# First attention of a two-layer kernel: scores as 32-row matmul tiles in pairs of PSUM banks

## The chip, the cores and the metric

The kernel runs on one core of one Trainium2 chip. The metric is device time in microseconds (us): the median of three runs before the change is 1856.27 us (1856.07 to 1857.29). TensorE is called PE below (its weight loads PEld), VectorE DVE, ScalarE ACT, GpSimd POOL. PSUM has eight banks here, each 128 partitions by 512 float32, addressed as `ps[:, bank, column]`.

## What is computed

Two transformer layers over x of 2048 tokens by 128 channels. Only the first sublayer is touched by the change, causal attention with 16 heads of 8 channels:

```python
q, k, v = (qkv[0], qkv[1], qkv[2])
q = _rms_norm(q, q_norm_w)
k = _rms_norm(k, k_norm_w)
q, k = _rope(q, k, cos, sin)
attn = jnp.einsum('bhqd,bhkd->bhqk', q, k) * scale
attn = jnp.where(causal, -jnp.inf, attn)
attn = jax.nn.softmax(attn, axis=-1)
out = jnp.einsum('bhqk,bhkd->bhqd', attn, v)
out = out.transpose(0, 2, 1, 3).reshape(Bc, Tc, C)
return out @ w_proj.T
```

It is followed by a linear frequency-domain layer, a linear attention, and a second softmax attention over experts (8 heads of 64 channels, not causal). Each adds its result to x.

## The kernel before

The tokens are 16 tiles of 128 (`NT`), in 4 chunks of 512 (`NC`, `CH`, `TPC` = 4 tiles a chunk). The 16 heads are taken in 4 groups of 4 (`NG`, `GH`). A head of 8 channels is staged into 32 columns: the value rounded, the rest that rounding left, and one column for the negated row maximum (`stageq`, `stagek`); four heads fill 128 columns. PE transposes a chunk of them into a bank and ACT copies it out (steps `k`, `q`, `q2`).

For queries one copy to `qT` is enough: head h lies in partitions 32h to 32h+31. Keys are copied to `kM[g % 2]`, which has a plane of 128 partitions for every head. Only the head's own 32 partitions hold values; the other 96 are zero, written once by POOL (`kM0`, `kM1`), so that a matmul over all 128 partitions gives the scores of one head. The copy takes four ACT instructions of 32 partitions (L862).

Every score is computed twice. The step `max` (L606, mask L609) computes scores of 128 queries by up to 512 keys, and DVE takes their maximum (L1074) into `mxp`; `m` combines them and `q2` transposes the queries again with the maximum in them. Then `S` (L623, mask L626) computes scores with keys in the partitions, two heads into two banks, and ACT takes exp of both banks in one instruction (L875) into `pbuf0`; `V` (L638) multiplies with the values, four heads in four 32-column tiles of PE into bank 6, each as two passes (float32); `O` copies bank 6 out, `F` transposes it, and DVE divides by the denominator. The causal mask is added by a bfloat16 matmul with the identity, one for each diagonal 128x128 block.

A unit is one `S` with its exp: 128 keys by up to 512 queries of two heads. There are 80 units a group, 320 in all: 192 off the diagonal with 512 columns, and 128 on it, with 512, 384, 256 or 128 columns (32 each). The `max` steps are 560: 384 off the diagonal with one 512-column matmul each, and 176 on it with 256 matmuls.

The order on all engines comes from one list, `SEQ0`, that `merge` builds: the units at their places, `V` for two units four units later, and the preparation for the coming group at places that `paced` interpolates. Each engine runs its own steps of that list strictly in order, with semaphore waits between them. Of the PSUM banks, `S` has 0 to 3 (two pairs in turn, `NS` = 2), bank 6 (`ACC`) gathers `V`, and `RING` = 4, 5, 7 is taken in turn by all else: the `max` steps, all transposes, `pj`, `mix`, `lin`. Before PE fills a bank, `take` waits until the step that had it last has been read. The second attention uses the same ring under the names `ring1` and `SEQ1`.

Chunk by chunk, as the last group ends, the steps `at`, `pj`, `sd`, `ln`, `lt`, `mix`, `sd2`, `ln2`, `lt2`, `lin`, `ex`, `el` carry the projection, the frequency layer and the inputs of the linear attention.

Of the kernel before, what the change touches and what calls it, by code (L numbers as in the profile page):

```python
# [25 lines left out]
ALU = mybir.AluOpType  # L26
# [23 lines left out]
RING = (4, 5, 7)  # L50
# [7 lines left out]
def preparation0():  # L58
# [5 lines left out]
    for g in range(NG):  # L64
# [7 lines left out]
        for c in range(NC):  # L72
# [69 lines left out]
class Ring:  # L142


    def __init__(self, seq, by_dve, by_act):
        self.turn, self.read, self.by_act, self.order = {}, {}, by_act, []
        counts = {True: 0, False: 0}
        for step in seq:
            if step[0] in by_dve + by_act:
                a = step[0] in by_act  # L150
                counts[a] += 1
                self.turn[step], self.read[step] = len(self.order), counts[a]
                self.order.append(step)

    def bank(self, step):
        return RING[self.turn[step] % len(RING)]


def build(nc, A):
    ctx = ExitStack()  # L160
    with ctx:
# [36 lines left out]
        masksb = s0("masksb", [P, 2, P], BF16)  # L198
# [38 lines left out]
        kM0 = s0("kM0", [P, GH, T], F32R)  # L237
        rotating = ExitStack()
        tmp = sbuf(rotating, "tmp", [P, NT, 2 * H0, D0])
        rotating.close()  # L240
        kM1 = s0("kM1", [P, GH, T], F32R)
        kM = (kM0, kM1)
# [71 lines left out]
        s_read1a = sem("s_read1a")  # L314
        s_m = sem("s_m")
# [96 lines left out]
        ring0 = Ring(SEQ0, ("max", "F", "pj", "mix", "lin"), ("k", "q", "q2", "at", "lt", "lt2"))  # L412
        ring1 = Ring(SEQ1, ("proj", "max", "F", "y"), ("t", "q2", "zt"))
# [123 lines left out]
        def _(pe):  # L537
# [32 lines left out]
            def take(ring, step):  # L570

                turn = ring.turn[step]
                if turn >= len(RING):
                    wait_read(pe, ring, ring.order[turn - len(RING)])
                return ring.bank(step)

# [7 lines left out]
            for step in SEQ0:  # L584
# [13 lines left out]
                elif kind == "max":  # L598
                    _, g, c, i, b, h, n = step
                    bank = take(ring0, step)  # L600
                    wait_read(pe, ring0, ("q", g, c))
                    wait_read(pe, ring0, ("k", g, b))
                    w = P * (i + 1) if b == c else CH
                    for a in range(n):
                        it = TPC * c + i
                        mm = pe.matmul(ps[:, bank, w * a:w * (a + 1)], qT[:, g % 2, P * it:P * (it + 1)],  # L606
                                       kM[g % 2][:, h + a, CH * b:CH * b + w], start=True, stop=b < c)
                        if b == c:
                            mm = pe.matmul(ps[:, bank, w * (a + 1) - P:w * (a + 1)], identb[:], masksb[:, 0, :],  # L609
                                           start=False, stop=True)  # L610
                    mm.then_inc(s_turn0, 1)
                elif kind == "S":
# [3 lines left out]
                    if u >= NS:  # L616
                        pe.wait_ge(s_exp, u - NS + 1)
                    wait_read(pe, ring0, ("q2", g, c))
                    wait_read(pe, ring0, ("k", g, c))
                    for i in range(2):  # L620
                        h = 2 * (u % 2) + i
                        b = 2 * (u % NS) + i
# [203 lines left out]
        def _(act):  # L826
# [22 lines left out]
            for step in SEQ0:  # L849
                kind = step[0]  # L850
                if kind in ("k", "q", "q2"):
# [5 lines left out]
                    if kind == "k":  # L857
                        if g == 1:
                            act.wait_ge(s_pconst, 2)
                        for h in range(GH):  # L860
                            rows = slice(32 * h, 32 * h + 32)
# [585 lines left out]
```

## Time and profile before

| | |
|---|---|
| time, median of 3 | 1856.27 us |
| span of the profiled execution | 1857.2 us |
| PE busy | 1645.3 us (89%) |
| DVE busy | 1435.4 us (77%) |
| POOL busy | 878.0 us (47%) |
| ACT busy | 782.5 us (42%) |
| chain that ended last, by engine | PE 66%, DVE 19%, issue 7%, POOL 5%, ACT 2% |
| of it, lines of the first attention | L606 8%, L623 7%, L638 7%, L581 5% |

The profiled execution's own time is its span, 1857.2 us, within 1 us of the median. Busy time of a PE matmul runs from its start to a modelled end, and the next one starts before that end; what a matmul costs is therefore the distance from its start to the next start. The exps of the first attention run from 74.4 us (unit 0) to 625.6 us (unit 319); the rest of the span, from there on, is work that the change leaves as it is.

### The profile page before, as it was taken

The page shows a single profiled execution, that of the slowest core. Times are in us where ns is not written, and L with a number is a line of the kernel's source. Part 1 is how long each engine was busy: PE and PEld are TensorE (multiplying, and loading weights), DVE is VectorE, ACT ScalarE, POOL GpSimd, SP SyncE. Part 2 cuts the span into 40 slices and gives each one's busy share as a digit, 9 for nine tenths or more (in the row PEclk, how much of TensorE's full clock was granted, in tenths as well). Part 3 has the DMA queues.
Part 4 walks back from the last instruction along what each step waited for, and adds up shares of the span by engine and source line. Part 5 has one row for each costly group of instructions (what it writes and reads, how often), then busy time and mean ns, then how long its engine had stood idle before and what let it go on. Part 6 is the DMA issues. An engine that isn't in the chain of part 4 may idle for free.

```text
span 1857.2 us, 26270 instructions
## 1 busy us (share of the span) xinstructions
PE 1645.3 (89%) x8612; PEld 999.3 (54%) x8612; DVE 1435.4 (77%) x2387; ACT 782.5 (42%) x1046; POOL 878.0 (47%) x906
## 2 busy tenths in 40 slices
PE   3899999999999672699899899899999899899997
PEld 2555555555554361566466466466565565565554
DVE  4996785785786369888888888888898888988862
ACT  3457557567556320223433434334334234234441
POOL 2710000000000024358678589589588587687654
PEclk9799999999999775889899999999999999999996
DMA  2000000000000000000000000000000000000000
GB/s 58 1 1 1 1 1 1 1 1 1 1 1 1 11 1 11 0 11 1 11 1 2 11 1 1 11 1 1 12 1 1 11 1 1 1 1 1 1 11 13
DMA packets 12224, 9.34 MB, mean 5 GB/s; under 512 B 3840, under 2 KB 11584, under 8 KB 12096
## 3 DMA queue, kind: packets, MB, share of 16 engines
q1 hardware_dynamic: 12096, 7.66, 1.5%
q8 instruction: 77, 1.26, 0.3%
q14 instruction: 51, 0.42, 0.1%
HBM read 6.61 MB, written 1.05 MB: 4 GB/s over the span
## 4 chain that ended last, share of the span: by engine, by line
PE 66%; DVE 19%; issue 7%; POOL 5%; ACT 2%; SPq 0%; DMA 0%; DVEq 0%; POOLq 0%; ACTq 0%
PE ps L786 10%; PE ps L606 8%; PE ps L623 7%; PE ps L638 7%; PE ps L759 6%; PE ps L581 5%; PE ps L775 4%; PE ps L776 4%; DVE den L1283 3%; PE ps L747 3%; DVE mxp L1256 3%; PE ps L749 2%; PE ps L748 2%; POOL z L1398 2%; PE ps L797 2%
## 5 line engine op out<-in xcount | busy, mean ns | idle before, releaser
L960 ACT ACTIVATE pbuf<-ps 128x1024 f32<-128x1024 f32 x256 | 262.1, 1024 | 524.0 <-PE ps L776 520.9
L1074 DVE TENSOR_REDUCE mxp<-ps 128x1 f32<-128x512 f32 (+3 forms) x560 | 354.2, 671 | 112.2 <-PE ps L606 56.2
L1256 DVE TENSOR_REDUCE mxp<-ps 128x1 f32<-128x512 f32 x512 | 342.5, 682 | 66.8 <-PE ps L759 66.1
L875 ACT ACTIVATE pbuf<-ps 128x1024 f32<-128x1024 f32 (+3 forms) x320 | 281.7, 896 | 199.1 <-PE ps L626 98.5
L1283 DVE TENSOR_TENSOR den<-den,pbuf 128x704 f32<-128x704 f32 x224 | 292.0, 1303 | 1.1
L786 PE MATMUL ps<-pbuf,h_v 128*64 128x512 f32 x1024 | 284.4, 634 | 0.0
L759 PE MATMUL ps<-k1T,q1T 128*128 128x512 f32 x512 | 223.4, 453 | 38.7 <-DVE mxp L1256 25.1
L1383 POOL TENSOR_TENSOR den<-den,pbuf 128x320 f32<-128x320 f32 x224 | 235.0, 1049 | 42.1 <-ACT pbuf L960 26.5
L606 PE MATMUL ps<-kM,qT 128*128 128x512 f32 (+3 forms) x640 | 243.6, 427 | 9.5 <-ACT kM L862 4.3
L1238 DVE TENSOR_TENSOR gt<-ps,gate 128x320 f32<-128x320 f32 x384 | 182.6, 484 | 54.8 <-PE ps L749 51.7
L623 PE MATMUL ps<-qT,kM 128*128 128x512 f32 (+3 forms) x640 | 207.7, 399 | 8.4 <-ACT pbuf L875 8.4
L775 PE MATMUL ps<-q1T,k1T 128*128 128x512 f32 x512 | 209.4, 409 | 2.3 <-ACT q2T L950 2.3
L776 PE MATMUL ps<-q2T,k2T 65*128 65x512 f32 x512 | 204.6, 400 | 0.0
L606 PEld LDWEIGHTS ps<-kM,qT 128*128 128x128 f32 x640 | 122.4, 197 | 118.7 <-DVE mxp L1074 88.7
L747 PE MATMUL ps<-wh,xh 128*128 128x320 f32 x384 | 136.1, 355 | 53.5 <-DVE gt L1238 36.9
L1367 POOL TENSOR_TENSOR gs<-gt 128x384 f32<-128x384 f32 x120 | 148.3, 1236 | 67.0 <-DVE gt L1238 65.3
L759 PEld LDWEIGHTS ps<-k1T,q1T 128*128 128x128 f32 x512 | 98.8, 194 | 146.3 <-DVE mxp L1256 87.0
L638 PE MATMUL ps<-pbuf,stagev 128*32 128x512 f32 (+3 forms) x1280 | 152.0, 547 | 0.0
L747 PEld LDWEIGHTS ps<-wh,xh 128*128 128x128 f32 x384 | 73.5, 191 | 142.1 <-DVE gt L1238 68.7
L1325 POOL TENSOR_SCALAR rstd<-meanvar 128x4 f32<-128x4 f32 x12 | 2.7, 227 | 304.5 <-DVE meanvar L995 304.5
L1340 POOL COPY stagev<-qkv 128x512 f32<-128x512 f32 x4 | 2.9, 722 | 288.8 <-PE ps L638 266.1
L623 PEld LDWEIGHTS ps<-qT,kM 128*128 128x128 f32 x640 | 117.9, 195 | 35.4 <-ACT pbuf L875 22.9
(212 smaller groups left out, 2484.3 us busy)
## 6 DMA issues: line engine op xcount, KB each, us to landing
wraw<-in_Wkv SPq DMA_DIRECT2D x16, 160.0 KB, 2.6
wraw<-in_Wq SPq DMA_DIRECT2D x8, 160.0 KB, 2.3
out<-x SPq DMA_DIRECT2D x4, 256.0 KB, 2.3
wqkv<-in_wqkvT SPq DMA_DIRECT2D x1, 192.0 KB, 4.0
masks<-in_masks SPq DMA_DIRECT2D x1, 128.0 KB, 4.1
dft<-in_dft SPq DMA_DIRECT2D x1, 128.0 KB, 2.3
wout<-in_Wo SPq DMA_DIRECT2D x2, 64.0 KB, 2.6
ident<-in_ident SPq DMA_DIRECT2D x1, 64.0 KB, 5.7
```

What stands on the lines that cost most here:

```text
L606: mm = pe.matmul(ps[:, bank, w * a:w * (a + 1)], qT[:, g % 2, P * it:P * (it + 1)], kM[g % 2][:, h + a, CH * b:CH * b + w], start=True, st ...
L623: mm = pe.matmul(ps[:, b, off:CH], kM[g % 2][:, h, P * jt:P * (jt + 1)], qT[:, g % 2, CH * c + off:CH * (c + 1)], start=True, stop=jt < TP ...
L638: mm = pe.matmul(ps[32 * h:32 * h + 32, ACC, off:CH], stagev[:, g % 2, jt, h, :], pbuf0[:, u % NP0, h % 2, off:CH], start=jt == 0, stop=jt ...
L747: pe.matmul(o, xh[:, t], wh[:, j, :], start=True, stop=False)
L759: pe.matmul(ps[:, bank, :], q1T[:, h % 2, P * it:P * (it + 1)], k1T[:, h % 2, CH * b:CH * (b + 1)], start=True, stop=True).then_inc(s_turn ...
L775: pe.matmul(ps[:, b, :], k1T[:, h % 2, t], q1T[:, h % 2, q], start=True, stop=False)
L776: mm = pe.matmul(ps[:, b, :], k2T[0:D1 + 1, h % 2, t], q2T[0:D1 + 1, h % 2, q], start=False, stop=True)
L786: mm = pe.matmul(ps[64 * i:64 * i + 64, ACC, :], h_v[:, h % 2, 2 * m + i, :], pbuf1[:, u % NP1, i, :], start=m == 0, stop=m == M1 - 1, til ...
L875: nc.scalar.activation(pbuf0[:, u % NP0, :, off:CH], ps[:, b:b + 2, off:CH], ACT.Exp, scale=float(D0) ** -0.5).then_inc(s_exp, 1)
L1074: v.tensor_reduce(mxp[:, i, h:h + n, b], ps[:, ring0.bank(step), 0:w * n].rearrange("p (h k) -> p h k", h=n), AX.X, ALU.max).then_inc(s_re ...
L1256: v.tensor_reduce(mxp1[:, it % TPC, b:b + 1], ps[:, ring1.bank(step), :], AX.X, ALU.max).then_inc(s_read1d, 1)
L1283: v.tensor_tensor(dn, dn, w, ALU.add).then_inc(s_den1, 1)
```

## The change

Keys are copied as they are, 128 partitions in one ACT instruction, to `kT0` and `kT1`; `kM0`, `kM1` and POOL's two memsets of them are gone. A score matmul takes the 32 partitions of its head alone (`tile_position=(rows.start, 0)`), for `S` and `max` both. `max` now treats two heads at once, in the two banks of a pair, and one DVE instruction reduces both banks (up to 1024 elements a partition). Banks 0 to 5 are three pairs that `S` and `max` take in one common turn (`Pairs`, `take_pair`, semaphores `s_pair0`, `s_max0`); bank 7 alone is left for all other steps (`SIDE0`). On the diagonal the masks of both heads follow the two score matmuls, and the first two query tiles share one step (`SEGMENTS`). The `max` steps become 288: 192 off the diagonal and 96 on it. The second attention keeps its ring as `RING1`. `tmp` no longer shares its place with `kM1`.

```diff
-RING = (4, 5, 7)
+SIDE0 = (7,)
+RING1 = (4, 5, 7)
+PAIRS0 = 3
+SEGMENTS = {1: ((0, 0), (1, P)), 2: ((2, 0),), 3: ((3, 0),)}
...
-            for i in range(TPC):
-                for b in range(c + 1):
-                    n = min(GH, TPC // (i + 1)) if b == c else 1
-                    items += [(("max", g, c, i, b, h, n), 1) for h in range(0, GH, n)]
+            for b in range(c + 1):
+                for i in range(b == c, TPC):
+                    items += [(("max", g, c, hp, b, i), 1) for hp in range(GH // 2)]
...
+class Pairs:
+    def __init__(self, seq):
+        self.order = [s for s in seq if s[0] in ("S", "max")]
+        self.turn = {s: i for i, s in enumerate(self.order)}
+        self.maxes = {s: i for i, s in enumerate(s for s in self.order if s[0] == "max")}
+    def bank(self, step):
+        return 2 * (self.turn[step] % PAIRS0)
...
+            def take_pair(step):
+                turn = pairs0.turn[step]
+                if turn >= PAIRS0:
+                    before = pairs0.order[turn - PAIRS0]
+                    if before[0] == "S":
+                        pe.wait_ge(s_exp, before[1] + 1)
+                    else:
+                        pe.wait_ge(s_max0, pairs0.maxes[before] + 1)
+                return pairs0.bank(step)
...
-                    for a in range(n):
-                        it = TPC * c + i
-                        mm = pe.matmul(ps[:, bank, w * a:w * (a + 1)], qT[:, g % 2, P * it:P * (it + 1)],
-                                       kM[g % 2][:, h + a, CH * b:CH * b + w], start=True, stop=b < c)
-                        if b == c:
-                            mm = pe.matmul(ps[:, bank, w * (a + 1) - P:w * (a + 1)], identb[:], masksb[:, 0, :],
-                                           start=False, stop=True)
-                    mm.then_inc(s_turn0, 1)
+                    for t, at in SEGMENTS[i] if b == c else ((i, 0),):
+                        it = TPC * c + t
+                        w = P * (t + 1) if b == c else CH
+                        for a in range(2):
+                            rows = slice(32 * (2 * hp + a), 32 * (2 * hp + a) + 32)
+                            mm = pe.matmul(ps[:, bank + a, at:at + w], qT[rows, g % 2, P * it:P * (it + 1)],
+                                           kT[g % 2][rows, CH * b:CH * b + w], start=at == 0, stop=b < c,
+                                           tile_position=(rows.start, 0), skip_group_check=b == c)
+                    if b == c:
+                        for a in range(2):
+                            for t, at in SEGMENTS[i]:
+                                mm = pe.matmul(ps[:, bank + a, at + P * t:at + P * (t + 1)], identb[:],
+                                               masksb[:, 1, :], start=False, stop=True, skip_group_check=True)
+                    mm.then_inc(s_pair0, 1)
...
-                        mm = pe.matmul(ps[:, b, off:CH], kM[g % 2][:, h, P * jt:P * (jt + 1)],
-                                       qT[:, g % 2, CH * c + off:CH * (c + 1)], start=True, stop=jt < TPC * c)
-                        if jt >= TPC * c:
-                            mm = pe.matmul(ps[:, b, off:off + P], identb[:], masksb[:, 1, :], start=False, stop=True)
+                        rows = slice(32 * (2 * (u % 2) + i), 32 * (2 * (u % 2) + i) + 32)
+                        mm = pe.matmul(ps[:, bank + i, off:CH], kT[g % 2][rows, P * jt:P * (jt + 1)],
+                                       qT[rows, g % 2, CH * c + off:CH * (c + 1)], start=True, stop=jt < TPC * c,
+                                       tile_position=(rows.start, 0))
+                    if jt >= TPC * c:
+                        for i in range(2):
+                            mm = pe.matmul(ps[:, bank + i, off:off + P], identb[:], masksb[:, 0, :],
+                                           start=False, stop=True)
...
-                        for h in range(GH):
-                            rows = slice(32 * h, 32 * h + 32)
-                            ins = nc.scalar.activation(kM[g % 2][rows, h, CH * c:CH * (c + 1)], ps[rows, b, :],
-                                                       ACT.Copy)
+                        nc.scalar.activation(kT[g % 2][:, CH * c:CH * (c + 1)], ps[:, b, :],
+                                             ACT.Copy).then_inc(s_read0a, 1)
...
+                    for t, at in SEGMENTS[i] if b == c else ((i, 0),):
+                        w = P * (t + 1) if b == c else CH
+                        ins = v.tensor_reduce(mxp[:, t, 2 * hp:2 * hp + 2, b], ps[:, bank:bank + 2, at:at + w],
+                                              AX.X, ALU.max)
+                    ins.then_inc(s_max0, 1)
...
-            g_.memset(kM0[:].bitcast(F32), 0.0).then_inc(s_pconst, 1)
...
-                    g_.memset(kM1[:].bitcast(F32), 0.0).then_inc(s_pconst, 1)
-                    pool.wait_ge(s_pconst, 2)
```

## Rows read from the trace of the kernel before

**Rows 1.** The page, part 1: busy time, share of the span, instructions of each engine.

```profile
PE 1645.3 (89%) x8612; PEld 999.3 (54%) x8612; DVE 1435.4 (77%) x2387; ACT 782.5 (42%) x1046; POOL 878.0 (47%) x906
```

**Rows 2.** Windows of 40, 20, 60, 20, (60), 20, 40, 20, 40 units.

```profile
core 0: us, PE busy (x) PEld busy (x) DVE busy (x) ACT busy (x) POOL busy (x), PEclk, DMA share, GB/s
74.40:153.50 79.10, 77.30 (x440) 42.57 (x440) 72.16 (x122) 38.60 (x45) 23.50 (x12) 1.00 0.00 1
153.50:193.40 39.90, 36.14 (x240) 20.99 (x239) 21.44 (x41) 29.71 (x42) 0.00 (x0) 0.96 0.00 1
193.40:288.60 95.20, 95.20 (x599) 51.98 (x598) 75.78 (x127) 55.44 (x66) 0.61 (x1) 1.00 0.00 1
288.60:328.20 39.60, 36.31 (x235) 21.77 (x234) 19.47 (x38) 29.68 (x42) 0.00 (x0) 0.91 0.00 1
...
423.40:462.40 39.00, 34.53 (x233) 20.38 (x232) 18.96 (x37) 29.60 (x43) 0.00 (x0) 0.96 0.00 1
462.40:527.70 65.30, 65.30 (x427) 36.22 (x425) 50.44 (x91) 37.59 (x47) 1.19 (x2) 1.00 0.00 1
527.70:568.80 41.10, 37.88 (x224) 21.78 (x223) 37.67 (x88) 21.96 (x29) 2.59 (x5) 1.00 0.00 1
568.80:625.60 56.80, 54.91 (x351) 27.34 (x354) 26.79 (x78) 39.09 (x52) 3.76 (x6) 1.00 0.01 1
```

**Rows 3.** Waits from 74 to 626 us: who waited for whom, us, times, longest.

```profile
PEld ps L606 <- DVE mxp L1074: 87.1, 133, 1.5
```

**Rows 4.** Timeline of PE: start us, us from first start to last end, instructions.

```profile
202.97 0.64 PE L638 MATMUL ps<-pbuf,stagev 128*32 128x512 f32 x4
...
263.77 0.36 PE L606 MATMUL ps<-kM,qT 128*128 128x256 f32 x1
263.98 0.23 PE L609 MATMUL ps<-masksb,identb 128*128 128x128 bf16 x1
...
265.77 0.63 PE L606 MATMUL ps<-kM,qT 128*128 128x512 f32 x2
266.24 0.62 PE L623 MATMUL ps<-qT,kM 128*128 128x512 f32 x2
...
269.09 0.39 PE L606 MATMUL ps<-kM,qT 128*128 128x512 f32 x1
269.41 1.06 PE L638 MATMUL ps<-pbuf,stagev 128*32 128x512 f32 x8
270.41 0.50 PE L606 MATMUL ps<-kM,qT 128*128 128x512 f32 x1
```

**Rows 5.** Groups by line and form (busy, mean ns, idle before), then a timeline row: DVE's reductions.

```profile
L1074 DVE TENSOR_REDUCE mxp<-ps 128x1 f32<-128x512 f32 x448 | 290.0, 686 | 68.3 <-PE ps L606 56.2 <-PE ps L609 9.1
...
L1027 DVE TENSOR_REDUCE ms<-tmp 128x192 f32<-128x1536 f32 x2 | 3.4, 1748 | 0.0
...
265.45 5.05 DVE L1074 TENSOR_REDUCE mxp<-ps 128x2 f32<-128x512 f32 x8 [0.44 <-PE ps L609]
```

**Rows 6.** ACT: two groups by form, then the timeline at a group's start.

```profile
L875 ACT ACTIVATE pbuf<-ps 128x1024 f32<-128x1024 f32 x224 | 224.9, 1024 | 129.0 <-PE ps L623 98.3 <-PE ps L626 29.8
L866 ACT ACTIVATE qT<-ps 128x512 fp32r<-128x512 f32 x32 | 19.0, 595 | 20.1 <-PE ps L581 19.9
...
160.57 4.80 ACT L862 ACTIVATE kM<-ps 32x512 fp32r<-32x512 f32 x8 [0.38 <-PE ps L581]
...
166.04 0.47 PE L623 MATMUL ps<-qT,kM 128*128 128x128 f32 x1 [2.56 <-ACT pbuf L875]
```

**Rows 7.** The lead-in before unit 0: a window, then a timeline row.

```profile
50.00:60.00 10.00, 5.94 (x25) 4.72 (x25) 9.01 (x9) 8.19 (x14) 1.39 (x1) 0.50 0.01 2
...
58.38 1.22 DVE L1074 TENSOR_REDUCE mxp<-ps 128x4 f32<-128x512 f32 x2
```

**Rows 8.** Timeline in the last units: DVE reads the bank of a `lin` step.

```profile
615.08 0.75 DVE L1126 TENSOR_SCALAR lt<-ps,bqcol 128x512 f32<-128x512 f32 x1 [3.73 <-PE ps L661]
615.75 0.74 DVE L1127 TENSOR_SCALAR lt<-ps,bqcol 128x512 f32<-128x512 f32 x1
```

More of the change, by code:

```diff
@@ L142, with __init__ @@
 class Ring:
-    def __init__(self, seq, by_dve, by_act):
-        self.turn, self.read, self.by_act, self.order = {}, {}, by_act, []
+    def __init__(self, seq, by_dve, by_act, banks):
+        self.turn, self.read, self.by_act, self.order, self.banks = {}, {}, by_act, [], banks
         counts = {True: 0, False: 0}
@@ L155, in bank @@
     def bank(self, step):
-        return RING[self.turn[step] % len(RING)]
+        return self.banks[self.turn[step] % len(self.banks)]
+class Pairs:
[5 more added lines that the diff above has]
+        return 2 * (self.turn[step] % PAIRS0)
 def build(nc, A):
@@ L235, in build @@
         linear.close()
[L237 to L242, printed above, removed]
+        kT0 = s0("kT0", [P, T], F32R)
+        tmp = s0("tmp", [P, NT, 2 * H0, D0])
+        s0("apart", [P, 2 * NT])
+        kT1 = s0("kT1", [P, T], F32R)
+        kT = (kT0, kT1)
         l0.close()
@@ L314, in build @@
         s_read1a = sem("s_read1a")
+        s_pair0 = sem("s_pair0")
+        s_max0 = sem("s_max0")
         s_m = sem("s_m")
@@ L411, in build @@
         SEQ1 = merge(by_place(preparation1() + after1), U1 * H1 + 16, foreground1)
-        ring0 = Ring(SEQ0, ("max", "F", "pj", "mix", "lin"), ("k", "q", "q2", "at", "lt", "lt2"))
-        ring1 = Ring(SEQ1, ("proj", "max", "F", "y"), ("t", "q2", "zt"))
+        ring0 = Ring(SEQ0, ("F", "pj", "mix", "lin"), ("k", "q", "q2", "at", "lt", "lt2"), SIDE0)
+        pairs0 = Pairs(SEQ0)
+        ring1 = Ring(SEQ1, ("proj", "max", "F", "y"), ("t", "q2", "zt"), RING1)
         def wait_read(eng, ring, step):
@@ L615, in _ @@
                     off = diag(c, jt)
-                    if u >= NS:
-                        pe.wait_ge(s_exp, u - NS + 1)
+                    bank = take_pair(step)
                     wait_read(pe, ring0, ("q2", g, c))
@@ L873, in _ @@
                         act.wait_ge(s_av, (u - NP0) // 2 + 1)
-                    b = 2 * (u % NS)
+                    b = pairs0.bank(step)
                     nc.scalar.activation(pbuf0[:, u % NP0, :, off:CH], ps[:, b:b + 2, off:CH], ACT.Exp,
@@ L1070, in _ @@
                 elif kind == "max":
-                    _, g, c, i, b, h, n = step
-                    wait_turn(dve, ring0, step)
-                    w = P * (i + 1) if b == c else CH
-                    v.tensor_reduce(mxp[:, i, h:h + n, b],
-                                    ps[:, ring0.bank(step), 0:w * n].rearrange("p (h k) -> p h k", h=n),
-                                    AX.X, ALU.max).then_inc(s_read0d, 1)
+                    _, g, c, hp, b, i = step
+                    dve.wait_ge(s_pair0, pairs0.maxes[step] + 1)
+                    bank = pairs0.bank(step)
+                    for t, at in SEGMENTS[i] if b == c else ((i, 0),):
[3 more added lines that the diff above has]
+                    ins.then_inc(s_max0, 1)
                     last = step
@@ L1079, in _ @@
                     _, g, c = step
-                    wait_read(dve, ring0, last)
+                    dve.wait_ge(s_max0, pairs0.maxes[last] + 1)
                     if g or c:
```

21 lines of the change are left out of this document (8 added, 13 removed).

## The prediction

> **What bounds the kernel now.** I read the page's busy shares first: PE 89%, DVE 77%, nothing else near [rows 1]. Shares over the whole span don't tell who is last in one stage, so the windows over the first attention come next, cut at exps of round unit numbers (0, 40, 60, 120, 140, 200, 220, 260, 280, end) [rows 2]. The reader is to see three kinds. In the long ones PE never rests: 95.2 of 95.2 us, with DVE at 75.8 and ACT at 55.4. There are two of 95.2 us (the second, from 328.2 to 423.4, differs by under 0.1 us and isn't shown) and a shorter one, 65.3 of 65.3. At the start of a group (153.5, 288.6 and 423.4 on, 39.0 to 39.9 us each) PE and ACT are both short of full, 36 and 30 us. In the first 40 units PE (77.3) and DVE (72.2) are both nearly full, as in the 20 units from 527.7, with 37.9 and 37.7 of 41.1. All together 551.2 us. Then the waits: PE's weight load of a `max` matmul waits for DVE 133 times, 87.1 us [rows 3], but the previous matmul is mostly still running meanwhile, which is why PE's busy time has no holes.
>
> **What a matmul costs.** The distance from start to start is the price [rows 4]. Two 512-column score matmuls at 265.77 and the next at 266.24: 0.47 us, so 0.23 each. A mask: 256-column matmul at 263.77, its mask at 263.98, so the 256 columns take about 0.12 plus an exposed weight load of 0.09, and the mask adds 0.04 to what follows. `V`: from 269.41 to the next at 270.41, 1.00 us. Its first four matmuls, one for each 32-column tile, lie within 0.64 us, hardly more than one of them lasts: tiles of one mode do run side by side. Into `V` the 512-column matmul at 269.09 took 0.32 instead of 0.23, so a change of tile mode costs about 0.09, and I take the same for leaving it.
>
> **Part 1, score matmuls in pairs (the large term).** There are 320 pairs in `S` and 320 in `max`: 192 and 192 of 512 columns, 128 and 128 of 512 to 128 columns. Two matmuls of a pair cost 2 x 0.23 = 0.46, or on the diagonal 2 x 0.147 (0.23, 0.176, 0.12 and 0.064 on average, worked out from the step of 0.23 for 512 columns). If the second head's tile starts at once, the second step goes: 384 x 0.23 + 256 x 0.147 = 126 us, less some 5 us for 640 late starts. No row shows two row tiles at work. The nearest is `V`'s four column tiles [rows 4], which start together; at the other end the two run one after the other and nothing is saved. I take side by side, since both heads write different banks and read different partitions, and keep 0 for the range. The Trainium skill (TensorE: Matmul & The Clock Gate, section "Measured speedup vs the span model") gives 3.07x for four row tiles of 512 columns, not 4x; a loss of 0.1 of a step for each tile after the first, read out of that, would leave some 12 of the 121 us on PE, an estimate from that page. No run here shows that yet.
>
> **Part 2, masks.** 512 stay. Before, each was covered by the matmul behind it but for 0.04. Now they stand in pairs or fours, each with its 128 columns (0.053 at the rate above); I take 0.06, so +10 us.
>
> **Part 3, changes of mode.** Counting the neighbours in the list of steps: now 320 changes (in and out of `V`), afterwards 773, since every diagonal step goes from row tiles to the full array for the masks and back, and so does each transpose. 453 x 0.09 = +41 us. Bounds: 0 if a full-array matmul can follow without a drain, and 0.2 each if row tiles drain worse than `V`.
>
> **PE's sum.** With these prices the PE work of units 0 to 319 comes to 445 us now and to 445 - 121 + 10 + 41 = 375 after. It takes 551, the rest being exposed weight loads and waits, so a factor of 1.24 overall and 1.15 in the long windows.
>
> **Part 4, DVE.** A 512-element maximum takes 0.63 us in a row of eight (5.05 / 8) though its record says 0.686 [rows 5]. 1536 elements took 1.748, so 1024 elements cost 0.686 + 512 x 1.037 ns = 1.22, back to back 1.17. Off the diagonal 192 x 1.17 = 225 against 384 x 0.63 = 242. On it each chunk and group took 11 instructions, 6.5 us; afterwards 8, of 256, 512, 768 and 1024 elements twice, 6.2. DVE loses 17 + 5 = 22 us in all, about 6 in each group. It does not halve.
>
> **Part 5, the key copy.** Four copies of 0.6 us become one of 0.6 (a copy of 32 partitions lasts as long as one of 128, 595 ns [rows 6]). 16 chunks, so 29 us less on ACT. At a group's start it is on the path: eight copies hold ACT for 4.80 us at 160.57, and PE then waits 2.56 us for an exp at 166.04 [rows 6].
>
> **Part 6, POOL.** Two memsets go. The first ends before the qkv copies do, the second is followed by nothing that waits for POOL until the next group. Nothing gained; the cover is that DVE is busy 9.0 of 10 us in the lead-in [rows 7], and if it were gone, the cost would still be nothing, since only work is removed.
>
> **Part 7, one side bank.** A transpose can start only when the one before it has been read. In a group's first units two of them stand close: `k` and `k`, `q` and `q`, and `F` right before `q`. While PE waits there, every `S`, `max` and `V` behind it waits. The reader needs 0.6 us (ACT) or two small DVE steps, behind an exp of 1.02 [rows 6]; I put 1 us on each of 8 such places that nothing covers (3 a group after the first, less one): +8. In the last units a second `lin` waits until DVE has read the first with two instructions of 0.75 [rows 8]: +1.5 at the very end.
>
> **Part 8, three shared pairs.** A turn waits for the reader three turns back. A cycle is weight load 0.1, matmul 0.40, the read (1.22 or 1.02), and 0.1 of signalling: 1.84 and 1.64 us per three turns. With one `max` per unit, six turns are three units, so at least 1.16 us a unit. Now a unit takes 95.2 / 60 = 1.59. It is under what DVE needs there and costs nothing by itself; behind DVE's other steps it can.
>
> **The sum by windows** [rows 2]. First 40 units: DVE 72.2 - 6 = 66 with 4 of waits, 70 against 79.1: -9. Three group starts: PE's floor is 24 us of 20 units, ACT 29.7 - 7.2 = 22.5, DVE about 20; I take 32 against 40: -24. Long windows (95.2 twice, 65.3): PE's work is 83.1 now and 70.3 after for 60 units, x 1.15 = 81, and DVE stands at 75.8 - 6.5 = 69; so close together that I take 84: -11, -11 and -7. From 527.7: DVE-bound, -1.5. The last 40 units: PE 54.9 busy, ACT 39.1, after it both near 45 with the `lin` steps between: -3. Lead-in -1 (DVE is busy 9.0 of 10 us there and comes to its first maxima at 58.38 [rows 7], so faster key copies bring little), end +1.5. That is -66; with Part 7's +8, -58. 1857.2 - 58 = 1799 in the span, and the median lies 0.9 below the span: **1798**.
>
> **Rivals.**
> *Readers and bank turns bind.* PE's gain is there, but the strict common turn couples ACT to DVE: an `F`, `m` or `stagek` on DVE holds a pair, then `S`, then exp. For it: PE's loads already wait 87.1 us for DVE [rows 3], and DVE sheds only 22 us. Against: 1.16 us against 1.59 a unit. Long windows would then fall by half of my value, group starts by 4 each: -15 - 12 - 9 + 8 = about -28, so 1828. The Trainium skill states this limit too (TensorEngine Tiling (Array Packing), section "PSUM Bottleneck"): tiling speeds up TensorE but not the reading of PSUM.
> *The two tiles don't overlap (slower).* Then the change doesn't do what it says. The saving of 121 goes, the 41 for modes and 10 for masks stay. 60 units of a long window have 122 pairs, +24 us on 70.3, so 94, x 1.1 = 104 against 95.2: +9, +9, +6; first 40 units +5, group starts 0 (ACT's gain against PE's loss), end +4: +33, so 1889. It decides from a second tile that starts later than 0.11 us after the first, half of the step of 0.23, where the 58 us are used up. Dear mode changes end there as well, from 0.22 each (453 x 0.13 = 58).
> *The clock falls.* In the lead-in, with PE busy 5.9 of 10 us, the granted clock was 0.50, which is 1.2 GHz; in the group starts it is 0.91 to 0.96 [rows 2, 7]. If a PE with more holes were granted 1.2 GHz for a good part of the stage, its 375 us would grow by over 100, and the time to about 1930. Against: PE stays the busiest engine with over 0.85.
> *No net change*: gains and stalls cancel, 1856.
>
> **How the numbers follow.** Forecast 0.64 (its own range 1783 to 1816), readers 0.17, no overlap or dear modes 0.11, clock 0.04, no change 0.04. The range reaches from 1777 (exposed loads fall more than in proportion) through the readers' case to 1852; what is left out is 0.03 below and 0.16 above. 0.2%, 3.7 us, is about what a measurement of this kernel tells from no change. Faster: 0.64 + 0.16 = 0.80; same 0.05; slower 0.15.
>
> **What the profile after would show.** Right: L606's successor and L623 start in twos within 0.02 us; PE's busy share in the long windows falls below 0.95; ACT's key copies take 0.6 us a chunk and the group starts shrink to 32 us; DVE's reductions show 1.22 us. Wrong in Part 1: second tile 0.23 us after the first. Wrong in Part 3: a mask over 0.15 us after the row tiles' end. Wrong in Part 7 or 8: PE's waits for ACT and DVE grow and its busy time drops while the windows keep their length. Everything after 625.6 us must keep its length; if it doesn't, the prediction misses from there.

## The result

The changed kernel takes 1929.5 us (median of 4, 1918.2 to 1952.8) against 1856.3: 1.037 times as long, 95% interval 1.034 to 1.041. The forecast was 1798 with a range up to 1852. On a second chip it took 1944.8 (1917.0 to 1961.0) against 1858.0. The ratios and intervals here leave out executions more than 1.5% above the fastest of their kernel, such as the one of 1952.8. The profiled execution has a span of 1931.5 us.

From the page of the kernel after, busy times and the granted clock of PE in 40 equal slices of the span (tenths of full speed):

```profile
PE 1685.6 (87%) x8612; PEld 926.1 (48%) x8612; DVE 1412.2 (73%) x2148; ACT 755.9 (39%) x998; POOL 864.5 (45%) x904
...
PEclk8558857555997977579989999999999999999997
```

DVE, ACT and POOL all shed work. PE, meant to lose most, is busy 40 us longer [rows 1], and its clock is down to 5 in six of the first ten slices. The windows of the same units as in [rows 2], again cut at the exps of units 0, 40, 60, 120, 140, 200, 220, 260, 280 and the last (columns as there: length, busy time and instructions of PE, PEld, DVE, ACT, POOL, then PE's clock):

```profile
76.30:170.80 94.50, 88.45 (x456) 34.47 (x460) 69.02 (x73) 38.80 (x45) 15.03 (x10) 0.61 0.00 1
170.80:201.60 30.80, 26.86 (x208) 11.77 (x208) 14.27 (x25) 22.09 (x30) 0.00 (x0) 1.00 0.00 1
201.60:323.80 122.20, 114.74 (x632) 42.17 (x632) 76.29 (x84) 56.91 (x68) 0.61 (x1) 0.65 0.00 1
323.80:358.60 34.80, 31.08 (x204) 13.24 (x200) 12.77 (x21) 21.94 (x31) 0.00 (x0) 0.79 0.01 1
358.60:495.40 136.80, 130.26 (x632) 46.10 (x632) 76.75 (x84) 57.22 (x68) 0.61 (x1) 0.54 0.00 1
495.40:524.10 28.70, 25.89 (x202) 11.82 (x198) 11.22 (x20) 21.54 (x30) 0.00 (x0) 1.00 0.00 1
524.10:592.40 68.30, 63.54 (x440) 26.05 (x444) 48.70 (x61) 38.46 (x49) 0.56 (x2) 0.90 0.00 1
592.40:640.00 47.60, 40.25 (x236) 17.63 (x232) 38.50 (x73) 21.78 (x29) 3.22 (x5) 0.78 0.00 1
640.00:697.00 57.00, 50.52 (x352) 20.77 (x356) 26.02 (x75) 38.35 (x51) 3.76 (x6) 0.97 0.01 1
```

| units | before | forecast | after | PE clock after |
|---|---|---|---|---|
| 0 to 39 | 79.1 | 70 | 94.5 | 0.61 |
| three group starts | 39.9, 39.6, 39.0 | 32 each | 30.8, 34.8, 28.7 | 1.00, 0.79, 1.00 |
| long windows | 95.2, 95.2, 65.3 | 84, 84, 58 | 122.2, 136.8, 68.3 | 0.65, 0.54, 0.90 |
| 260 to 279 | 41.1 | 39.6 | 47.6 | 0.78 |
| 280 to 319 | 56.8 | 54 | 57.0 | 0.97 |

Unit 0 starts 1.9 us later, and from the last exp to the end it is 1234.5 us against 1231.6. In all 15.4 - 24.2 + 71.7 + 6.5 + 0.2 + 1.9 + 2.9 = 74 us more. The time follows the last column of the table. Two group starts at full clock (30.8 and 28.7) and the end of the stage at 0.97 (57.0) are within 3.3 us of the forecast; the window with the lowest clock lost most. The 2.9 us after the last exp are not the change's: two more profiled executions of the changed kernel or nearly it (after_again, after_spaced) have 1231.7 and 1230.8 there.

A window holds the same units before and after, but not quite the same work: the new order of the `max` steps takes some out of the group starts (240 matmuls before, 208 after in the first) and puts them into the long windows (599 before, 632 after).

PE was not idle before its clock fell. Three windows of 5 us of the kernel after:

```profile
215.00:220.00 5.00, 4.56 (x34) 1.77 (x30) 2.75 (x5) 3.04 (x5) 0.00 (x0) 1.00 0.01 2
220.00:225.00 5.00, 4.55 (x34) 1.50 (x32) 4.35 (x4) 3.76 (x5) 0.00 (x0) 0.96 0.00 0
225.00:230.00 5.00, 5.00 (x26) 1.96 (x22) 1.67 (x2) 2.00 (x3) 0.00 (x0) 0.50 0.00 0
```

PE is busy for 91% of each of the first two, and after the fall, with the clock at 1.2 GHz (0.50), for all of the third; in the windows at 0.54 to 0.65 it is busy for 93 to 95%. Compare the lead-in before the change, where 0.50 went with PE 59% busy [rows 7].

The timeline of PE at full clock, kernel after (start, length, instructions):

```profile
541.46 0.50 PE L653 MATMUL ps<-qT,kT 32*128 32x512 f32 x2
541.79 0.40 PE L635 MATMUL ps<-kT,qT 32*128 32x512 f32 x2
542.12 0.28 PE L641 MATMUL ps<-masksb,identb 128*128 128x128 bf16 x2
542.34 0.50 PE L653 MATMUL ps<-qT,kT 32*128 32x512 f32 x2
542.77 0.28 PE L658 MATMUL ps<-masksb,identb 128*128 128x128 bf16 x2
```

And at half clock:

```profile
265.00 1.94 PE L671 MATMUL ps<-pbuf,stagev 128*32 128x512 f32 x8
266.87 0.81 PE L653 MATMUL ps<-qT,kT 32*128 32x512 f32 x4
```

The two matmuls of a pair (x2) do run side by side: both within 0.50 us, where one alone lasts 0.50 with its load. In the last row even four start together, since two units of `S` stand next to each other and use all four strips. From the pair at 541.46 to the next it is 0.33 us, not 0.23; what makes the difference is read further down, under "Part 1, pairs". `V` costs 1.00 at full clock [rows 4] and 1.87 at half.

### The profile page after: what moved, and what is told of

It is laid out like the page before. It is cut to its first block, busy times and chain, and to the rows that moved or that the text cites. A ratio compares the mean times of both kernels' runs of the same rounds, so it can differ in the third digit from the quotient of the medians.

```text
span 1931.5 us, 25707 instructions
## 1 busy us (share of the span) xinstructions
PE 1685.6 (87%) x8612; PEld 926.1 (48%) x8612; DVE 1412.2 (73%) x2148; ACT 755.9 (39%) x998; POOL 864.5 (45%) x904
## 4 chain that ended last, share of the span: by engine, by line
PE 64%; DVE 20%; issue 7%; POOL 5%; ACT 3%; SPq 0%; DMA 0%; DVEq 0%; POOLq 0%; ACTq 0%
PE ps L819 10%; PE ps L671 9%; PE ps L792 6%; PE ps L608 6%; PE ps L635 5%; PE ps L653 5%; PE ps L808 4%; PE ps L809 4%; DVE mxp L1105 4%; DVE den L1314 3%; PE ps L780 3%; DVE mxp L1287 3%; PE ps L782 2%; PE ps L781 2%; ACT pbuf L903 2%
## 5 line engine op out<-in xcount | busy, mean ns | idle before, releaser
L1105 DVE TENSOR_REDUCE mxp<-ps 128x2 f32<-128x1024 f32 (+2 forms) x320 | 329.9, 1062 | 195.5 <-PE ps L635 122.4
L988 ACT ACTIVATE pbuf<-ps 128x1024 f32<-128x1024 f32 x256 | 262.2, 1024 | 523.6 <-PE ps L809 520.7
L671 PE MATMUL ps<-pbuf,stagev 128*32 128x512 f32 (+3 forms) x1280 | 198.2, 700 | 0.7 <-ACT oT L911 0.7
L635 PE MATMUL ps<-kT,qT 32*128 32x512 f32 (+3 forms) x640 | 178.4, 592 | 16.5 <-ACT pbuf L903 10.8
L653 PE MATMUL ps<-qT,kT 32*128 32x512 f32 (+3 forms) x640 | 167.4, 554 | 20.5 <-DVE mxp L1105 17.0
L653 PEld LDWEIGHTS ps<-qT,kT 32*128 32x128 f32 x640 | 70.5, 229 | 136.5 <-DVE mxp L1105 67.1
L635 PEld LDWEIGHTS ps<-kT,qT 32*128 32x128 f32 x640 | 73.8, 244 | 122.5 <-ACT pbuf L903 43.8
```

The source lines that it names most:

```text
L635: mm = pe.matmul(ps[:, bank + a, at:at + w], qT[rows, g % 2, P * it:P * (it + 1)], kT[g % 2][rows, CH * b:CH * b + w], start=at == 0, stop ...
L653: mm = pe.matmul(ps[:, bank + i, off:CH], kT[g % 2][rows, P * jt:P * (jt + 1)], qT[rows, g % 2, CH * c + off:CH * (c + 1)], start=True, st ...
L671: mm = pe.matmul(ps[32 * h:32 * h + 32, ACC, off:CH], stagev[:, g % 2, jt, h, :], pbuf0[:, u % NP0, h % 2, off:CH], start=jt == 0, stop=jt ...
L1105: ins = v.tensor_reduce(mxp[:, t, 2 * hp:2 * hp + 2, b], ps[:, bank:bank + 2, at:at + w], AX.X, ALU.max)
```

## The experiments

Theory A: the clock falls because the score matmuls use only one or two of the array's four 32-row strips. Theory B: the new bank turns leave pauses in PE's work, and these lower it. Beside the clock, each run prices a part of the change. The ratios are to the kernel before on the same chip; times of two runs may come from two chips, on which the kernel before took 1855.4 to 1858.0.

**full_rows.** The changed kernel with zero-padded keys and score matmuls over all 128 rows again. The key copy is again four instructions and POOL's memsets are back, as before the change. The edit in `max`; `S` has the same:

```diff
-                            rows = slice(32 * (2 * hp + a), 32 * (2 * hp + a) + 32)
-                            mm = pe.matmul(ps[:, bank + a, at:at + w], qT[rows, g % 2, P * it:P * (it + 1)],
-                                           kT[g % 2][rows, CH * b:CH * b + w], start=at == 0, stop=b < c,
-                                           tile_position=(rows.start, 0), skip_group_check=b == c)
+                            h = 2 * hp + a
+                            mm = pe.matmul(ps[:, bank + a, at:at + w], qT[:, g % 2, P * it:P * (it + 1)],
+                                           kM[g % 2][:, h, CH * b:CH * b + w], start=at == 0, stop=b < c,
+                                           skip_group_check=b == c)
...
```

> The changed kernel with its score matmuls back on the whole array (zero-padded keys, 128 rows), all else as changed: bank pairs in a common turn, one side bank, maxima over two banks. Theory A (the clock falls because score matmuls hold only one or two 32-row strips of the array): mean granted clock back to 0.94, time 1860 to 1880, the excess over 1856 being the price of bank turns and side bank. Theory B (it falls because the new turns leave holes in PE's work): clock stays at 0.86 to 0.88, time 1930 or more, since the streaming is longer too.

Measured: 1911.9 us, 1.028 times before (1.023 to 1.033), clock 0.944. The clock is back, so the turns did not lower it: A. But the time is 30 us above what A allowed. The new banks and the new order of steps together, with four key copies as before, cost about 50 us.

**half_rows.** 64-row tiles: head h in the lower half beside head h+2 in the upper, zeros in the other head's rows, four key copies. The rows in `max`; `S` has the same halves:

```diff
-                            rows = slice(32 * (2 * hp + a), 32 * (2 * hp + a) + 32)
+                            h = hp + 2 * a
+                            rows = slice(64 * a, 64 * a + 64)
...
```

> The changed kernel with 64-row tiles: a pair is head h in rows 0 to 63 and head h+2 in rows 64 to 127, the other head's 32 rows of each half zero, so that two matmuls still run side by side and together cover all 128 rows. The key copy is again four instructions. Theory A: clock 0.93 or more, and with PE's saving kept the time is 1800 to 1825. Theory B: clock 0.86 to 0.88, time 1915 to 1940 as in the changed kernel.

Measured: 1881.4 us, 1.011 times (1.007 to 1.016), clock 0.927. The clock as A said, but 56 us or more above its time.

**quarter_rows.** half_rows with one line changed for each of `max` and `S`.

```diff
-                            rows = slice(64 * a, 64 * a + 64)
+                            rows = slice(32 * h, 32 * h + 32)
```

> half_rows with one edit: each score matmul takes the 32 rows of its head instead of the 64 rows of its half, same buffers, pairs, order and instruction count. If the share of the array's rows in use decides the clock, it falls from 0.93 to 0.86 to 0.88, and the time rises from 1881 to 1925 to 1950. If the clock follows the pauses and mode changes, which are the same in both, clock and time stay at 0.93 and 1881.

Measured: 2016.9 us, 1.086 times (1.081 to 1.091), clock 0.819. The same 60 units (140 to 199) in both, first half_rows, then quarter_rows (columns as in the windows above):

```profile
334.80:432.90 98.10, 88.37 (x632) 35.71 (x632) 75.80 (x84) 56.74 (x68) 0.62 (x1) 0.97 0.00 1
```

```profile
404.60:541.50 136.90, 130.26 (x632) 46.08 (x632) 76.82 (x85) 57.33 (x69) 0.62 (x1) 0.54 0.00 1
```

Equal instruction counts, equal work on DVE and ACT, but clock 0.97 against 0.54 and 39 us. PE's busy share rises, from 0.90 to 0.95. One edit, the rows of the score tiles, made this difference, and it went beyond A's range (1925 to 1950). Around the start of these 60 units, half_rows:

```profile
328.00:333.00 5.00, 2.37 (x18) 0.83 (x16) 1.98 (x2) 4.29 (x6) 0.00 (x0) 1.00 0.00 0
333.00:338.00 5.00, 4.74 (x22) 1.70 (x20) 2.93 (x3) 1.94 (x2) 0.00 (x0) 0.52 0.00 0
...
343.00:433.00 90.00, 81.17 (x598) 33.08 (x598) 71.51 (x82) 52.27 (x64) 0.62 (x1) 1.00 0.00 1
```

And quarter_rows:

```profile
395.00:400.00 5.00, 2.46 (x14) 1.07 (x10) 1.23 (x1) 3.17 (x5) 0.00 (x0) 0.82 0.00 0
...
405.00:410.00 5.00, 5.00 (x24) 1.69 (x28) 2.45 (x2) 2.26 (x4) 0.00 (x0) 0.50 0.00 0
410.00:529.00 119.00, 114.23 (x528) 40.09 (x524) 65.48 (x68) 47.66 (x57) 0.62 (x1) 0.50 0.00 1
```

In both the clock falls behind a pause, with PE busy about 2.4 of 5 us. So Theory B has its part: here a pause starts the low clock. What the rows decide is how long it lasts: with all rows in use it is back at full clock from 343 on, with half of them it stays at 0.50 for more than 119 us, with PE busy for 96% of them. What the pair doesn't tell is whether the rows count that a pair covers or the height of its tiles: a pair of 64-row tiles covers all 128 rows, a pair of 32-row tiles 64 of them, and no run keeps four 32-row tiles at work throughout.

**tiles_S.** The kernel before, its `S` alone in 32-row tiles.

```diff
-                        mm = pe.matmul(ps[:, b, off:CH], kM[g % 2][:, h, P * jt:P * (jt + 1)],
-                                       qT[:, g % 2, CH * c + off:CH * (c + 1)], start=True, stop=jt < TPC * c)
+                        rows = slice(32 * h, 32 * h + 32)
+                        mm = pe.matmul(ps[:, b, off:CH], kM[g % 2][rows, h, P * jt:P * (jt + 1)],
+                                       qT[rows, g % 2, CH * c + off:CH * (c + 1)], start=True, stop=jt < TPC * c,
+                                       tile_position=(rows.start, 0))
```

> The kernel before with one edit: the matmuls of S take the 32 rows of their head (same zero-padded key buffer, same banks, rings and order). Theory A: clock between the two kernels, 0.88 to 0.92, time 1865 to 1900. Theory B: the rings of before keep PE fed, clock 0.94, and half of the streaming saved on S gives 1820 to 1845.

Measured: 1971.3 us, 1.058 times (1.050 to 1.065), clock 0.932 in the profiled execution and 0.896 to 0.927 in the others, against 0.942 to 0.948 for the kernel before. Both theories missed the time, A by 71 us and B by 126. The clock is between the two kernels, as A had it, though nearer to the kernel before. Units 200 to 259, then 10 us of them, then the stretch behind these:

```profile
520.20:617.20 97.00, 97.00 (x427) 42.61 (x427) 51.88 (x91) 38.48 (x47) 1.27 (x2) 0.77 0.00 1
...
549.60:559.60 10.00, 10.00 (x56) 5.00 (x59) 6.09 (x10) 3.05 (x6) 0.00 (x0) 1.00 0.00 0
560.00:604.00 44.00, 44.00 (x144) 17.96 (x138) 18.83 (x32) 13.26 (x17) 0.00 (x0) 0.50 0.00 1
```

PE is busy without a hole, and the clock falls to 0.50 for 44 us all the same. No pause starts it here, so Theory B alone can't be right. These 60 units took 65.3 us before. Together with units 40 to 59 (50.5 us at 0.76) and 260 to 279 (50.3 at 0.83) they make 52 of the 100 us that the profiled execution is longer. The two other long windows, at full clock, give 17.6 each (112.8 against 95.2). The timeline of PE shows what costs time there:

```profile
229.87 0.49 PE L606 MATMUL ps<-kM,qT 128*128 128x512 f32 x1
230.30 0.50 PE L624 MATMUL ps<-qT,kM 32*128 32x512 f32 x2
230.72 0.50 PE L606 MATMUL ps<-kM,qT 128*128 128x512 f32 x1
...
231.59 0.50 PE L624 MATMUL ps<-qT,kM 32*128 32x512 f32 x1
232.01 0.23 PE L628 MATMUL ps<-masksb,identb 128*128 128x128 bf16 x1
232.18 0.50 PE L624 MATMUL ps<-qT,kM 32*128 32x512 f32 x1
232.61 0.23 PE L628 MATMUL ps<-masksb,identb 128*128 128x128 bf16 x1
232.65 0.48 PE L606 MATMUL ps<-kM,qT 128*128 128x512 f32 x1
```

A pair alone in its mode costs 0.42 us to the next full-array matmul (230.30 to 230.72), and the `max` matmul before it 0.43 instead of 0.23. That is 0.85 where three full-array matmuls cost 0.69: the pair's side-by-side gain of 0.23 is gone in one round trip, and 0.16 more. On the diagonal, where a mask stands between the two heads, they don't overlap at all: 1.06 us (231.59 to 232.65), against 0.71 for the same four matmuls in the kernel before (155.38 to 156.09). A pair alone between full-array matmuls doesn't pay; where several stand together it can, as the rows under "Part 1, pairs" show.

**half_offdiag.** half_rows with the diagonal steps back on the whole array.

```diff
-                        rows = slice(64 * i, 64 * i + 64)
+                        rows = slice(64 * i, 64 * i + 64) if jt < TPC * c else slice(0, P)
```

> half_rows with the diagonal steps back on the whole array, so that a mask follows its score matmul without a change of mode; 64-row tiles only off the diagonal. Counted in the list of steps, changes between score tiles and whole array fall from 455 to 289. If such a change costs 0.1 us on top of the weight load that it exposes (0.2 in all), and a diagonal pair 0.05 more on the whole array, PE's sum falls by 16 us and the time from 1881 to 1862 to 1872. If changes cost 0.09, as forecast, the two effects cancel and it stays at 1881 or rises by up to 10.

Measured: 1888.9 us, 1.017 times (1.014 to 1.020), clock 0.931: 8 us slower than half_rows, the second case. In the 60 units from 140 PE is busy 94.2 us (88.4 in half_rows) of 100.8 (98.1). So fewer changes of mode gave nothing that the lost overlap on the diagonal didn't take back. In the kernel after, a pair and its mask (542.34 to 542.77) take 0.43, a pair and the next pair (541.46 to 541.79) 0.33: 0.10 for what follows the pair, near the 0.09 of the forecast.

**two_pairs.** full_rows with two pairs in the common turn and three side banks.

```diff
-SIDE0 = (7,)
-PAIRS0 = 3
+SIDE0 = (4, 5, 7)
+PAIRS0 = 2
```

> full_rows with its banks dealt otherwise: two pairs in the common turn of S and max instead of three, and three side banks (4, 5, 7) instead of one. If the common turn is what costs full_rows its 50 us over the kernel before, this gets much worse, 1960 or more. If the single side bank costs them, it gets better, 1870 to 1890.

Measured: 2026.2 us, 1.091 times (1.088 to 1.095), clock 0.938. 114 us over full_rows, the first case: one pair less in the common turn costs 114 us more than two more side banks give back. As both were changed at once, the run prices neither alone, and it doesn't show how the 50 us of full_rows divide. PE's own waits for the readers of the pairs (engine, line, for whom: us, times, longest):

```profile
PEld ps L636 <- DVE mxp L1110: 142.5, 161, 4.0
PE ps L636 <- DVE mxp L1110: 73.5, 108, 3.8
PEld ps L654 <- ACT pbuf L908: 68.6, 73, 3.0
```

**one_side.** The kernel before with the side steps in bank 7 and the one-head `max` steps in 4 and 5.

```diff
-        ring0 = Ring(SEQ0, ("max", "F", "pj", "mix", "lin"), ("k", "q", "q2", "at", "lt", "lt2"))
+        ring0 = Ring(SEQ0, ("F", "pj", "mix", "lin"), ("k", "q", "q2", "at", "lt", "lt2"), (7,))
+        maxes = {s: i for i, s in enumerate(s for s in SEQ0 if s[0] == "max")}
...
+                    bank = 4 + maxes[step] % 2
```

> The kernel before with the side steps confined to bank 7 and the one-head max steps in banks 4 and 5 by turns, S keeping its own two pairs; nothing else. It prices the single side bank and the shallower ring without a common turn. If these cost full_rows its excess: 1885 to 1910. If the common turn of S and max does: 1858 to 1870.

Measured: 1933.4 us, 1.042 times (1.037 to 1.047), clock 0.941, more than either case had. Two of its waits:

```profile
PEld ps L611 <- DVE mxp L1079: 141.3, 252, 2.4
...
PE ps L584 <- ACT kM L867: 15.0, 7, 2.8
```

The loads' wait for DVE is up from 87 [rows 3] to 141 us, and transposes wait up to 2.8 us for the key copy before them. Both the side steps and `max` had lived on three banks in common, and dividing these costs time even without a common turn with `S`. How much of the 77 us is the side bank and how much the two-deep ring, this run doesn't part.

**half_two_copies.** half_rows with two scaled key copies of 128 partitions.

```diff
-                        for h in range(GH):
-                            rows = slice(32 * h, 32 * h + 32)
-                            ins = nc.scalar.activation(kM[g % 2][rows, h, CH * c:CH * (c + 1)], ps[rows, b, :],
-                                                       ACT.Copy)
+                        for h in range(2):
+                            ins = nc.scalar.activation(kM[g % 2][:, h, CH * c:CH * (c + 1)], ps[:, b, :],
+                                                       ACT.Copy, scale=own[:, h:h + 1])
```

> half_rows with the key copy in two ACT instructions of 128 partitions, each scaled by a column of ones and zeros so that the other head's rows become zero, instead of four of 32; POOL's memsets go. If the key copies hold the single side bank at a group's start, where PE of half_rows waits up to 2.2 us for it, each of the three group starts gives 4 to 6 us, the lead-in 1 to 2: 1881 becomes 1861 to 1869. If other readers hold it, 1876 to 1881.

Measured: 1848.0 us (10 executions; before on that chip 1855.4), 0.995 times (0.992 to 0.998), clock 0.936. More than expected: 33 us below half_rows. By windows of the profiled executions (27 us apart), the three group starts give 21 of it (41.0, 41.6, 40.2 become 34.4, 34.5, 32.5), and a part of it is the clock, which in these starts goes from 0.88, 0.82 and 0.83 to 0.95, 0.90 and 0.95. How much the copies give at equal clock is not shown.

**half_spaced.** half_two_copies with each `q` and `k` placed apart among the `max` items.

```diff
-        out += [(("stagek", g), 3), (("k", g, 0), 1), (("k", g, 1), 1)]
+        out += [(("stagek", g), 3), (("k", g, 0), 1)]
...
-            if c + 1 < NC:
-                out.append((("q", g, c + 1), 1))
-            if c + 2 < NC:
-                out.append((("k", g, c + 2), 1))
...
+            if c + 1 < NC:
+                items.insert(3, (("k", g, c + 1), 1))
+                items.insert(1, (("q", g, c + 1), 1))
```

> half_two_copies with the side steps of a group spread in the list: one k at the start instead of two, each later q and k put after the first and third max items of the chunk before, so that no two transposes stand side by side. If the single side bank costs by steps that stand close (a forecast of 1 us a place, more by the trace), this gives another 5 to 15 us: 1850 to 1862. If what PE waits for is the common turn of the pairs, it stays within 3 us of half_two_copies.

Measured: 1841.3 us, 0.992 times (0.988 to 0.995), clock 0.939. Faster than both kernels; against the kernel before by 0.5 to 1.2%, clear of noise, but small. Against half_two_copies the medians say 7 us and the intervals overlap, so the side bank's share is likely, not shown; of the 12.1 us between the two profiled executions the three group starts have 10.5 (34.4, 34.5, 32.5 become 30.6, 30.6, 29.7). The window of units 140 to 199:

```profile
312.80:406.80 94.00, 84.61 (x626) 34.94 (x626) 72.69 (x79) 57.76 (x71) 0.62 (x1) 1.00 0.00 1
```

Full clock, PE busy 10.6 us less than before, and 9.4 us in which it waits. 95.2 became 94.0.

**after_spaced.** The same spreading in the changed kernel.

> The same spreading of side steps in the changed kernel with its 32-row tiles and single copy. Fewer pauses, same rows in use. If the rows in use decide the clock, it stays at 0.85 to 0.88 and the time within 10 us of the changed kernel's 1930 to 1945; if pauses decided, the clock would rise above 0.90 and the time fall below 1900.

Measured: 1913.8 us, 1.028 times (1.023 to 1.034), clock 0.867. Somewhat more time back than expected (1920 or more), 16 us below the changed kernel's first median, with the clock where A put it: 0.867 to 0.882 in its four executions.

**after_again.** The changed kernel once more, on a second chip.

> The changed kernel again on the same chip as the other runs of this call. Both theories: clock 0.85 to 0.88, time 1915 to 1955, with a spread of 1 to 2% between executions where the kernel before shows 0.1%.

Measured: 1944.8 us (1917.0 to 1961.0), clock 0.848 to 0.872, the median as expected. The spread is 2.3%, and on this chip the kernel before spread by 0.9% (1854.9 to 1871.7), not by the 0.1% of the first set.

## Why the prediction was wrong, point by point

**The clock (a rival at 0.04).** It is what turned the sign. The step that failed is the argument against this rival, "PE stays the busiest engine with over 0.85"; the sum has no term for the clock and takes every price from rows at full clock. Busy share didn't decide. At full clock PE was busy 0.91 before the clock fell at 225 in the kernel after, and without a hole before the fall in tiles_S, while windows of half_rows and half_two_copies kept 0.97 and 1.00 at a busy share of 0.90. half_rows against quarter_rows shows 136 us for the rows in use. The lead-in had tempted me to read the low clock as a matter of pauses [rows 7]; what the change did to the array was the one thing about it that no row of before could show, and that called for a larger chance. The changed kernel, which differs from half_two_copies in the rows in use and in one key copy less, is 85 us above it (1931.5 and 1846.4, spans).

That the rival's time, 1930, falls on the measured 1929.5 is luck. It laid the blame on "a PE with more holes", and it set its 100 us and more on top of the forecast's gain of 58, of which little was there.

**Part 1, pairs.** The mechanism was right, and so was the price for pairs that follow one another. The second matmul starts within 0.02 us, as forecast. A row of three pairs on the same two halves in half_two_copies, at full clock, with the weight loads (PEld) of the second and third:

```profile
207.50 0.50 PE L654 MATMUL ps<-qT,kM 64*128 64x512 f32 x2
207.61 0.19 PEld L636 LDWEIGHTS ps<-kM,qT 64*128 64x128 f32 x2
...
207.85 0.40 PE L636 MATMUL ps<-kM,qT 64*128 64x512 f32 x2
207.85 0.19 PEld L654 LDWEIGHTS ps<-qT,kM 64*128 64x128 f32 x2
208.08 0.40 PE L654 MATMUL ps<-qT,kM 64*128 64x512 f32 x2
...
208.41 0.28 PE L659 MATMUL ps<-masksb,identb 128*128 128x128 bf16 x2
```

The first pair comes after other work, so its record of 0.50 has its own load in it, and it is 0.35 us to the second. The second was loaded while the first ran, its record is 0.40, and it is 0.23 to the third: two matmuls in the time of one. From the third to a mask it is 0.33. So a pair costs 0.23 within a row of pairs, 0.10 more where its own load stands open, and 0.10 more where a mask or `V` follows. The Trainium skill (TensorE: Matmul & The Clock Gate, section "The mechanism") says that a weight load overlaps a running matmul only where the row groups differ. This trace doesn't agree: the loads at 207.61 and 207.85 go to the same halves as the pair that runs, and the measurement decides.

What the sum missed is how seldom a load is hidden. Of the 512-column pairs at full clock in half_two_copies, 323 of 421 have their own load in their record; in the kernel before it is 371 of 882 matmuls. The factor of 1.15 let the open loads shrink with the work, and they hardly did.

**Part 2, masks.** 0.06 forecast. Two masks and what stands before the next pair take 0.22 us (542.12 to 542.34); less the 0.09 of an open load, 0.065 each. Right.

**Part 3, changes of mode.** 0.09 each was right to 0.01 or 0.02, as the prices in Part 1 show. half_offdiag fits, but as the overlap on the diagonal went with the changes, it doesn't price them alone.

**Part 4, DVE.** 1.22 us forecast for 1024 elements, measured in the kernel after (busy us, mean ns):

```profile
L1105 DVE TENSOR_REDUCE mxp<-ps 128x2 f32<-128x1024 f32 x216 | 258.8, 1223 | 141.1 <-PE ps L635 122.4 <-PE ps L641 17.2
```

The total is right too: DVE sheds 23 us where 22 were forecast. Its place is not. The forecast took 6.5 us off each long window, and they stayed at 75.8 before and 76.3 and 76.8 after; the group starts lost 21.6 together, as `max` steps moved from there into the long windows. DVE still never bound the long windows: 76.3 us of 122.

**Part 5, key copy.** The number was right: the three group starts give 24.2 us against 24 forecast, one of them at a clock of 0.79. The cause is only in part the one forecast, since the starts also hold fewer `max` steps than before. full_rows, with four copies, the same steps and whole-array matmuls, has 43.0, 42.4 and 39.0 there, more than the kernel before.

**Part 6, POOL.** Nothing to see, as said. The lead-in lost 1.9 us where I had put a gain of 1, at a clock of 0.50 before and after (50 to 60 us).

**Parts 7 and 8, banks.** Mis-sized, and by more than the range allowed for: I booked 8 us for the side bank, 3 a long window for the turns. full_rows carries about 50 us, masks and order among them; one_side shows 77 for another way to deal six banks. The working of Part 8 took a unit's mean of 1.16 (its terms add up to 1.15) against 1.59 us and found slack; but the steps are not even, and PE, strictly in order, waits at each uneven place. In the long window of half_two_copies, at full clock, it still waits 9.6 us:

```profile
319.60:415.50 95.90, 86.26 (x632) 34.97 (x632) 75.65 (x84) 56.51 (x68) 0.62 (x1) 1.00 0.00 1
```

**The sum again.** Over units 0 to 319 the windows of the profiled executions give this:

| | time, us | PE busy | PE waits |
|---|---|---|---|
| before | 551.2 | 532.8 | 18.4 |
| full_rows | 592.3 | 541.4 | 50.9 |
| half_two_copies | 537.3 | 478.4 | 58.9 |

PE's gain was there, 54 us where the sum had 445 - 375 = 70. The waits took 41 of them back, where some 17 were booked (8 for the side bank, 3 in each of three long windows). half_two_copies, which keeps most of the clock (0.936), ends at -11 us in the span (1846.4 against 1857.2), near the *no net change* case. The 85 us that the rows in use and the key copy make then give the 74 us of the changed kernel. The rival in which tiles don't overlap is refuted by every timeline. The readers' rival, 1828 at full clock, comes nearest to what half_spaced measures, 1841.

What stays open: how the 50 us of full_rows divide between common turn, side bank, key copies and masks; whether four 32-row tiles at once would hold the clock; and whether 64-row tiles hold it everywhere, since half_rows still shows 0.82 in one group start.

## What to carry to other kernels

Cutting the rows of a zero-padded matmul saves no time by itself, only what runs beside it does, and a PE that uses fewer of its rows can lose its clock while it looks fully busy. Read the granted clock per stage beside the busy share, and try tiles that together still cover all rows; here two of 64 rows did. Price a tiled matmul with its weight load in the open unless another of the same mode stands right before it, and count the changes of mode. Banks that steps had in common are not free to divide: every other deal of them tried here cost 50 us or more on whole-array matmuls, so measure a new deal apart from the change that it serves.

## What was unexpected of the hardware

- The granted clock depends on the rows that the matmuls use: 0.54 with 32-row pairs, 0.97 with 64-row pairs in the same 632 matmuls, PE busier in the slower one.
- The clock fell to 0.50 for 44 us behind 10 us in which PE had no hole at all (tiles_S, 32-row pairs between whole-array matmuls).
- Executions of the changed kernel spread by 1.8 and 2.3% on two chips (1918 to 1953 us, 1917 to 1961), those of the kernel before by 0.1% in the first set and up to 0.9% later.
- The weights of a pair load while another pair runs on the same rows: 0.23 us from pair to pair, as for one whole-array matmul.
- An ACT copy with a scale column of ones and zeros takes 0.686 us, against 0.595 for a plain one [rows 6]. Two of them (1.37 us) replace four (2.4 us). From the groups of half_two_copies by shape, from 78 us to 615 us of its span (busy us, mean ns, idle before and what ended it):

```profile
L893 ACT ACTIVATE kM<-ps,own 128x512 fp32r<-128x512 f32 x24 | 15.2, 686 | 1.8 <-PE ps L609 1.5
```
